# Slot experts: gates applied as a token's two rows are summed, by diagonal matrices on TensorE, and half of the shared experts' products placed behind the tiles

## The reference, cut to what matters

```
gates  = softmax(xf @ router_w)                      # 14 routed experts
masked = the two largest gates of a token, others 0
masked = masked / (masked.sum(-1) + 1e-9)
routed = silu(rms(x) @ W1[e]) @ W2[e]                # hidden width 256
x = layernorm(x + sum_e masked[e] * routed[e] + sum of 2 shared experts)
```

## Time and profile before

| | |
|---|---|
| time, median of 3 runs | 1085.94 us (1085.79 to 1091.52) |
| profiled execution, its own time | 1087.3 us |
| its span, first to last instruction | 1085.5 us |
| mean granted TensorE clock | 0.922 |
| busy: PE, DVE, ACT, POOL | 88%, 72%, 54%, 39% |

### The profile page before, as it was taken

One profiled execution on the slowest core, in us unless ns is written; L12 is line 12 of the kernel. 1 busy time (PEld: TensorE's weight loads), 2 busy tenths in 40 slices (PEclk: granted clock), 3 DMA queues, 4 the chain that ended last, 5 costly groups with the idle time before them and its releaser, 6 DMA issues.

```text
span 1085.5 us, 17936 instructions
## 1 busy us (share of the span) xinstructions
PE 959.6 (88%) x5387; PEld 802.4 (74%) x5387; DVE 778.1 (72%) x2002; ACT 586.0 (54%) x1375; POOL 421.4 (39%) x490
## 2 busy tenths in 40 slices
PE   6999999999997799995884768887979999999994
PEld 5899999999984557773663658785657888888883
DVE  4666666666668672441788999935759999999995
ACT  3666666666656632444575333324656555555554
POOL 3566666666654412554540747643381000000001
PEclk8999999999998698997897688886989999999998
DMA  6232323222314101341101222001006666566551
GB/s 245 72 103 89 100 82 106 82 99 87 109 65 155 40 10 28 85 79 49 30 20 40 78 79 78 1 1 45 14 1 162 173 173 165 171 180 175 165 145 39
DMA packets 46979, 98.29 MB, mean 91 GB/s; under 512 B 7106, under 2 KB 23170, under 8 KB 45779
## 3 DMA queue, kind: packets, MB, share of 16 engines
q1 hardware_dynamic: 44466, 92.64, 27.8%
q0 software_dynamic: 2464, 5.05, 2.4%
HBM read 75.25 MB, written 22.41 MB: 90 GB/s over the span
## 4 chain that ended last, share of the span: by engine, by line
PE 42%; issue 19%; POOL 18%; DVE 15%; ACT 4%; DMA 1%; SPq 1%; POOLq 0%; DVEq 0%; ACTq 0%
PE PS L1783 8%; PE PS L1784 8%; PE PS L1785 8%; POOL P L661 7%; POOL WS L670 3%; PE PS L1979 3%; DVE r0b L1589 3%; POOL WS L666 2%; DVE rb L1602 2%; PE PS L1993 2%; PE PS L1928 1%; PE PS L2135 1%; PE PS L1934 1%; DVE dfb L1594 1%; ACT Xp L443 1%
## 5 line engine op out<-in xcount | busy, mean ns | idle before, releaser
L661 POOL TENSOR_TENSOR P<-P,rl 128x256 f32<-128x256 f32 (+1 forms) x130 | 104.8, 827 | 121.2 <-DVE rl L1220 121.2
L436 POOL TENSOR_TENSOR rs<-ms,neghalf 128x4 f32<-128x4 f32 (+1 forms) x28 | 26.0, 928 | 304.1 <-DVE nm L430 303.9
L1213 DVE CUSTOM_DVE_ANT_0 P<-PS,cmask 128x128 f32<-128x128 f32 (+1 forms) x260 | 77.1, 352 | 70.6 <-issue 70.5
L1138 ACT ACTIVATE FG<-PS 128x512 f32<-128x512 f32 x112 | 67.0, 598 | 103.3 <-PE PS L1785 103.3
L882 ACT ACTIVATE P<-P,mn 128x128 f32<-128x128 f32 (+1 forms) x260 | 114.3, 444 | 1.9 <-DVE mn L1213 1.9
L1783 PE MATMUL PS<-XTh,W 128*128 128x512 f32 x256 | 102.3, 399 | 0.8
L1784 PE MATMUL PS<-XTl,W 128*128 128x512 f32 x256 | 101.1, 395 | 0.0
L1785 PE MATMUL PS<-XTh,W 128*128 128x512 f32 x256 | 101.1, 395 | 0.0
L1854 PE MATMUL PS<-VO,PT 128*128 128x128 f32 x804 | 100.6, 275 | 0.0
L1854 PEld LDWEIGHTS PS<-VO,PT 128*128 128x128 f32 x804 | 95.0, 192 | 0.0
L1769 DVE TENSOR_TENSOR FU<-FG,PS 128x512 f32<-128x512 f32 x112 | 77.0, 688 | 23.3 <-PE PS L1785 23.3
(11 more groups left out here) (449 smaller groups left out, 2660.7 us busy)
## 6 DMA issues: line engine op xcount, KB each, us to landing
GI<-coef SPq DMA_DIRECT2D x56, 256.0 KB, 4.1
GW<-coef SPq DMA_DIRECT2D x56, 256.0 KB, 4.1
w3s<-WS SPq DMA_DIRECT2D x32, 384.0 KB, 2.6
W<-w3s SPq DMA_DIRECT2D x32, 384.0 KB, 3.3
Wb<-decay SPq DMA_DIRECT2D x7, 1024.0 KB, 4.6
WR<-in_w SPq DMA_DIRECT2D x32, 192.0 KB, 2.5
WR<-in_w SPq DMA_DIRECT2D x16, 256.0 KB, 2.8
w12f<-WS SPq DMA_DIRECT2D x16, 256.0 KB, 2.1
```

What stands on the lines that cost most here:

```text
L661: last = pool.tensor_tensor(v, v, f, ALU.mult)
L1138: act.activation(FG[:, k % 2, :], bank(4 + k % 2), ACT.Silu).then_inc(sem("fg_done"), 1)
L1213: dve.tensor_tensor_reduce(out=P[:, slot, c:c + w], in0=scores(par, q), in1=cmask[:, 256 - w:256], scale=1.0, scalar=3e38, op0=ALU.add, op ...
```

## The change

1. The gates leave the slots. `gslot`, `gated_hot` and the 32 gate products go, and `slot_out` is a plain copy. The gates of a token (`gAB`, one for each of its two rows) are applied as its rows are summed. DVE writes the matrices `eqP[s, t]` = identity times gate (`gate_matrix`, 28 of them, for pairs 1 to 7), and `pair_sum` multiplies GA and GB by those in place of the identity, each tile of 128 columns apart. For pair 0 DVE multiplies and adds in four `scalar_tensor_tensor`.
2. The 14 remaining gate steps and the 28 gate matrices stand in the slot loop, one step or two matrices an iteration, from iteration 6 to 33. Gate steps 0 and 1 stand ahead of the ranks, and the Exp on ACT at step 5.
3. The shared experts go by chunks. Chunks 0 and 1 (8 up, 8 down products) stay ahead of the slot loop, chunks 2 and 3 come behind it, with their transposes and additions. `slot_tokens` stands at steps 5 and 6, two groups each.
4. The context's products and copies move ahead, into the cross attention of layer 0, where the norms of the queries are computed.
5. The four `dsel` go from ahead of the token stage into it: `selector(b - 1)` behind `pair_norm(b + 2)` for b = 1 to 4.
6. Buffers are laid out anew, so that what the second half of the shared products reads is not overwritten.

The diff, cut: the body of `gates_step` is the same in both and left out, and so are the declarations.

```diff
-        RANKS_AT, HOT_AT = 0, (5, 6, 8, 9)
+        GATES_EXP = 5
+        RANKS_AT, HOT_AT = 0, {5: (0, 1), 6: (2, 3)}
...
+            act.wait_ge(sem("ctx_pe"), CTX_PE["ke_ready"])
+            act.activation(kTe[:, :], bank(0), ACT.Copy).then_inc(sem("ctx_act"), 1)
+            act.wait_ge(sem("ctx_pe"), CTX_PE["ve_ready"])
+            act.activation(vE[:, :, :], bank(1, CH, 2)[0:64, :].rearrange("p (b d) -> p b d", b=B), ACT.Copy).then_inc(sem("ctx_act"), 1)
+            act.wait_ge(sem("ctx_pe"), CTX_PE["kk_ready"])
+            act.activation(KK[:, :], bank(3), ACT.Copy, scale=1.0 / math.sqrt(D)).then_inc(sem("ctx_act"), 1)
...
-            for n in range(16):
+            def shared_silu(n):
                 act.wait_ge(sem("up_ready"), n + 1)
                 if n >= 4:
                     act.wait_ge(sem("down_done"), n - 3)
                 act.activation(Hf[:, n % 4, :], bank(4 + n % 2), ACT.Silu).then_inc(sem("sg_done"), 1)
+
+            def shared_sum(c):
+                act.wait_ge(sem("down_done"), 4 * c + 4 if c >= 2 else 8)
+                act.activation(OT[:, c * CH:c * CH + CH], bank(c), ACT.Copy).then_inc(sem("sums_out"), 1)
+
+            for n in range(8):
+                shared_silu(n)
                 if n == GATES_EXP:
                     act.wait_ge(sem("lg_sub"), 1)
                     act.activation(Lg[:, :, :], Lg[:, :, :], ACT.Exp).then_inc(sem("lg_exp"), 1)
-            act.wait_ge(sem("gslot_done"), on("gslot_done", 1))
...
                     act.wait_ge(sem(f"ys_out{j % RING}"), on(f"ys_out{j % RING}", j // RING * 16))
-                act.activation(Y[j % RING][:, :], slot_y, ACT.Copy, scale=gslot[:, j:j + 1]).then_inc(sem("yt_done"), 1)
...
 
             for i in range(NT + 3):
-                if i < NC_:
-                    act.wait_ge(sem("down_done"), 16)
-                    act.activation(OT[:, i * CH:i * CH + CH], bank(i), ACT.Copy).then_inc(sem("sums_out"), 1)
+                if i < 2:
...
 
+            for n in range(8, 16):
+                shared_silu(n)
+                if n == 14:
+                    shared_sum(2)
+            shared_sum(3)
...
-            act.wait_ge(sem("sel32_done"), 1)
-            for b in range(4):
+
+            def selector(b):
+                act.wait_ge(sem("sel32_done"), 1)
                 act.activation(dsel[b][:, :, :], sel32[:, 8 * b:8 * b + 8].rearrange("p (h o) -> p h o", o=1).to_broadcast([64, H1, 128]),
                                ACT.Copy).then_inc(sem("dsel_done"), 1)
 
...
+                if b <= 4:
+                    selector(b - 1)
...
-            for n in range(2, 16):
-                gates_step(n)
-            after_last()
-            for s in range(2):
-                dve.tensor_tensor(eqJ[:, s, :, :], eqJ[:, s, :, :], bt(gAB[:, s, :], NT), ALU.mult).then_inc(sem("gated_hot"), 1)
-            dve.wait_ge(sem("gates_ready"), 1)
-            dve.tensor_copy(gslot[:, :], SLOT_GATE).then_inc(sem("gslot_done"), 1)
+
+            def gate_matrix(t):
+                for s in range(2):
+                    dve.tensor_scalar(eqP[:, s, t, :], ident[:, :], gAB[:, s, t:t + 1], None, ALU.mult).then_inc(sem("diag_done"), 1)
+
+            def add_shared(c, b):
+                dve.wait_ge(sem("sums_T"), c + 1)
+                x = Xp[:, S + c * CH:S + c * CH + CH]
+                dve.tensor_tensor(x, x, bank(b), ALU.add).then_inc(sem("shared_added"), 1)
...
+                if 6 <= i < 20:
+                    gates_step(i - 4)
+                if i == 20:
+                    after_last()
+                if 20 <= i < 20 + T - 2:
+                    gate_matrix(i - 18)
...
-                    x = X[:, 0:2, :]
                     dve.wait_ge(sem("ya_in0"), on("ya_in0", 64))
-                    dve.tensor_tensor(x, x, GA[:, 0:2, :], ALU.add).then_inc(sem("first_sum"), 1)
-                    dve.wait_ge(sem("first_sum"), 1)
-                    dve.tensor_tensor(x, x, GB[:, 0:2, :], ALU.add).then_inc(sem("first_sum"), 1)
-                    dve.wait_ge(sem("first_sum"), 2)
+                    for s, y in enumerate((GA, GB)):
+                        if s:
+                            dve.wait_ge(sem("first_sum"), 2)
+                        for t in pair(0):
+                            dve.scalar_tensor_tensor(X[:, t, :], y[:, t, :], gAB[:, s, t:t + 1], X[:, t, :], ALU.mult, ALU.add).then_inc(sem("first_sum"), 1)
+                    dve.wait_ge(sem("first_sum"), 4)
...
+            pe.wait_ge(sem("l1_in"), 16 * 7)
+            pe.wait_ge(sem("q_act"), NC_ + 1)
+            pe.matmul(bank(0), wqe[:, 0, :], ctxT[:, :], start=True, stop=True).then_inc(sem("ctx_pe"), 1)
+            pe.wait_ge(sem("q_act"), NC_ + 3)
+            for b in range(B):
+                last = pe.matmul(bank(1 + b // 4)[0:64, b % 4 * 128:b % 4 * 128 + 128], ctxT[:, b * SC:b * SC + SC], wqe[:, 0, :],
+                                 start=True, stop=True)
+            last.then_inc(sem("ctx_pe"), 1)
...
+                    pe.wait_ge(sem("ctx_act"), CTX_ACT["ke_done"])
+                    pe.wait_ge(sem("q_act"), NC_ + 4)
+                    pe.matmul(bank(3), wqe[:, 1, :], kTe[:, :], start=True, stop=True).then_inc(sem("ctx_pe"), 1)
+            pe.wait_ge(sem("ctx_act"), CTX_ACT["kk_done"])
 
...
-                e, c, m = n // 8, n // 2 % 4, n % 2
+                c, e, m = n // 4, n // 2 % 2, n % 2
                 if n >= 2:
                     pe.wait_ge(sem("sg_done"), n - 1)
                 else:
                     pe.wait_ge(sem("chosen_done"), on("chosen_done", n + 1))
+                if n == 8:
+                    pe.wait_ge(sem("xt_done"), on("xt_done", NT))
+                    pe.wait_ge(sem("hs_done"), on("hs_done", NT))
                 pe.matmul(bank(4 + m), WS0[:, e, m * 128:m * 128 + 128], XTs[:, c * CH:c * CH + CH],
                           start=True, stop=True).then_inc(sem("up_ready"), 1)
 
...
+            def shared_T(c, b):
+                pe.wait_ge(sem("sums_out"), c + 1)
+                for t in tiles(c):
+                    last = pe.transpose(bank(b)[:, t % 4 * 128:t % 4 * 128 + 128], OT[:, t * 128:t * 128 + 128], ident[:, :])
+                last.then_inc(sem("sums_T"), 1)
...
-                if n in HOT_AT:
-                    slot_tokens(HOT_AT.index(n))
+                for g in HOT_AT.get(n, ()):
+                    slot_tokens(g)
...
-            for s in range(2):
-                pe.wait_ge(sem("gated_hot"), on("gated_hot", s + 1))
-                for t in range(T):
-                    last = pe.matmul(SLOT_GATE, eqP[:, s, t, :], eqJ[:, s, t, :], start=s == 0 and t == 0,
-                                     stop=s == 1 and t == T - 1, skip_group_check=True)
-            last.then_inc(sem("gates_ready"), 1)
             pe.wait_ge(sem("te_done"), on("te_done", 1))
-            pe.wait_ge(sem("gslot_done"), on("gslot_done", 1))
...
+                    shared_T(i - 2, i - 2)
+
+            for n in range(8, 16 + 2):
+                if n < 16:
+                    shared_up(n)
+                if n >= 10:
+                    shared_out(n - 2)
+            pe.wait_ge(sem("shared_added"), on("shared_added", 2))
+            for c in range(2, NC_):
+                shared_T(c, c - 2)
             pe.wait_ge(sem("l1_split"), 5)
...
-                for n, y in enumerate((X, GA, GB)):
-                    last = pe.matmul(sum2(b), ident[:, :], y[:, 2 * b:2 * b + 2, :].rearrange("p t d -> p (t d)"), start=n == 0, stop=n == 2)
+                pe.wait_ge(sem("diag_done"), on("diag_done", 4 * b))
+                pe.matmul(sum2(b), ident[:, :], X[:, 2 * b:2 * b + 2, :].rearrange("p t d -> p (t d)"), start=True, stop=False, skip_group_check=True)
+                for t in pair(b):
+                    for s, y in enumerate((GA, GB)):
+                        last = pe.matmul(part(sum2(b), t), eqP[:, s, t, :], y[:, t, :], start=False, stop=s == 1, skip_group_check=True)
                 last.then_inc(sem("y_sum"), 1)
```

160 lines of the change are left out of this document (70 added, 90 removed).

## The result

The changed kernel took 1073.8 us (median of 4 runs, 1069.35 to 1076.47) against 1085.87 for the kernel before in the same job: ratio 0.9868, 95% interval 0.9841 to 0.9894. It is faster by 12.1 us, clear of the noise, where 21.5 were forecast, and its time lies 2.3 us above the forecast's range. Two later jobs timed the same kernel again: 1069.05 us (6 runs, 1064.66 to 1070.41, ratio 0.981, 0.9782 to 0.9837) and 1066.46 us (5 runs, 1065.54 to 1068.42, ratio 0.9809, 0.9788 to 0.983). So the first job's four runs were its slow end. The two later jobs ran on different chips, and the first job's chip is not on record, so a share of that can be the chip's. Twelve of fifteen runs lie at or under 1071.5, and the gain is 18.5 to 22 us in the later jobs. What was wrong, and what was only bad luck of one execution, has to be read from parts.

A forecast was written before the change was run, and what follows sets the result against it. PE bounds the slot loop; ACT, DVE and GpSimd close the token stage's loop. Terms 23.2 + 1.2 - 1.0 + 1.3 - 3.2 = 21.5 us, against the median 1085.94, gave 1064.5 us; 8-in-10 range 1058.5 to 1071.5.

The forecast's parts named there:

- The start of the slot loop, 23.2 us: Ahead of the slot loop: it starts 23.2 us earlier, by gate products 9.0, sixteen shared products 13.8, `gslot` wait 0.5.
- this rival: Ahead of the slot loop: PE's clock falls over narrow products, costing about 4 us, 1068.5 us in all; chance 0.12.
- The loop, 1.2 us: Slot loop: 1.2 us gained as PE comes from dense work and two of four transpose sets are gone.
- VectorE's work is free: Slot loop: one gate step or two matrices an iteration fit in DVE's 0.90 us idle, at zero cost.
- The tail, -1.0: Behind the slot loop: ACT copies the last shared sum before norming pair 0, so 1.0 us is given back.
- The token products of tile 0, +1.3: Up to DVE's first token-stage work: PE comes from 14 us of products, not idleness, so 1.3 us gained.
- The selectors, -3.2: Token stage's closed loop: three selectors cost 0.97 us each and the fourth 0.3, together 3.2 us lost.
- Behind 594 us, 0 with 1 either way: Behind 594 us: nothing changes but the phase of PE's clock, between 1 us either way.

The follow-up runs named there:

- spread groups: Changed kernel with one `slot_tokens` group behind each of four product pairs, not two behind two: 1066.75 us; spread also in runs of 1077.09 and 1064.93 us.
- the filler's: Changed kernel plus three 512-column products with unused results on PE behind pair 0's transposes: 1067.65 us, ratio 0.9807.
- the three edits together: Changed kernel with `slot_tokens` groups set apart, two unused products ahead of the first slot transpose, and selectors in the shared products' second half: 1064.93 us, ratio 0.9785.

## Why the prediction was wrong, and where it was right

*The start of the slot loop, 23.2 us: failed by the clock.* This is the step that failed: that PE runs two groups, two shared products in 1.79 us, and two groups again, all at full clock. It was right in order and wrong in price. The two shared products took 3.48 us in the first profile, and the ones behind the second pair were slow too; 20.3 us came in place of 23.2. With the same instructions and the clock up, 23.2 came, of which the loop lost 0.7 again, where PE waited 0.53 us for rows. I gave this rival 0.12, on the ground that four groups with products between them had lost nothing before. That ground was good for single groups (the clock held in all three runs with spread groups, and in the kernel before) and not for two together, where it fell in eight profiles of ten. The rival's row was in my own table: 9 us of narrow products and a fall within them. I had priced it at 4 us; 2.9 came. The Trainium skill, "TensorE: Matmul & The Clock Gate", "What's actually happening", says that the clock goes by how busy PE has been; by the first profile's busy time PE was busy all of 387 to 391 us at 0.57, so read in that way the rule does not hold here. Why the clock held in two of the ten is open.

*The loop, 1.2 us: mis-sized to the low side, then lost.* It is 3.2 to 3.3 us shorter in the clean profiles. The copy without its multiplier, priced at zero, gives 1.4 to 1.5 of it. The rest, 1.8, is for the most part the loop's start at a higher clock, for which 1.2 had stood together with the transposes; these are worth 0.3 at most. In the first profile the pauses took 3.8 us and turned the term's sign. VectorE's work is free, as forecast.

*The tail, -1.0: right* (-0.9 in all profiles of the changed kernel). It holds thanks to the context's move, worth 5 us here. The prediction took the context's work out of this place and asked what it costs elsewhere, and not what it would have cost to leave it.

*The token products of tile 0, +1.3: right* in two profiles of three (+1.4), and the loss of 0.6 in the first hangs on the pause at 491. But it is nearly all given back on the way to tile 1, at the lower clock, in 1.2 us more than before. The prediction followed the clock no further than tile 0.

*The selectors, -3.2: right.* The stage lost 3.5 to 3.8. From PROD to PROD, the third profile against the one before, the four turns with a selector are longer by 0.8, 0.9, 0.9 and 0.3 us, 2.9 together: three near 0.97 and the fourth at 0.3, as forecast. The first turn adds the clock's 1.2, and the second takes 0.6 less. Moving the selectors gives 2.5 back and leaves the first turn's 1.2. It is not `pair_sum`.

*Behind 594 us, 0 with 1 either way: too narrow.* From the last PRZ to the last scan all fourteen profiles have 111.3 to 111.8 us. From there to the end they have 384.1 to 388.8, though no kernel changes anything there. In 705 to 750 us the granted clock was 0.70 in the run with 388.6 and 0.81 in the one with 384.2 (the filler's), and a share of what is won ahead comes and goes here. That this depends on where the clock stands when the stage is reached is my guess; it was not tried.

Against the profile of before, the sum was 21.5 us. The three executions gave 13.7, 18.2 and 21.8. What put the first one out of the range is, beside the clock's 2.9, the pauses: 3.8 us in the loop and, with the lower clock that follows, 2.0 behind it. The clock's 2.9 alone would have left the time within the range, as it did in both later jobs. The other three runs of the first job, 1069.35 to 1076.47 us, left no trace, so whether they had pauses is not known. The third execution's 21.8 is in part luck: 1.9 us of it come from a first group at 382.4 in place of 384.3, ahead of all that the sum is about, and the loop's 2.0 above its term make up for most of the clock's 2.9.

The cause of the pauses is open. ScalarE and VectorE both wait for PE then, so it is PE or what feeds it. VectorE's new work is unlikely: the pauses at 404 and 491 us lie outside 409.9 to 453.6 us, where its gate steps and matrices run, and in the third profile they run with no pause. The ring of Y, of four tiles, is unlikely too: between 424 and 445 us a tile's write lands 1.9 to 2.9 us after its issue in the second profile, and its place is asked for some 5.5 us after that issue; the first profile does not show these landings. No experiment brought the pauses back, and so none could take them away.

The best versions are the one with the selectors in the second half (1063.38) and the three edits together (1064.93). Both beat the kernel before clearly; against the changed kernel (0.981) their 0.9783 and 0.9785 overlap in the intervals, so by times they are not shown to be faster than it; the 2.5 us of the token stage are seen in their profiles.
